# Query convolution in plain fp32, and values of two kv heads on two column halves

## What is computed

```python
qkv = x @ w_qkv.T
q = qkv[..., :LATENT]          # 1024 channels, 16 heads of 64
k = qkv[..., LATENT:LATENT + KV_DIM]   # 256 channels, 4 kv heads
q = _causal_conv1d(_causal_conv1d(q, qc1_w, qc1_b, N_HEADS), qc2_w, qc2_b, 1)
k = _causal_conv1d(_causal_conv1d(k, kc1_w, kc1_b, N_KV), kc2_w, kc2_b, 1)
...
q = _rope(_l2norm(q + 0.5 * k_mean), cos, sin)
k = _rope(_l2norm(k + 0.5 * q_mean) * key_temp, cos, sin)
attn = jax.nn.softmax(jnp.where(causal, q @ kg.T * scale, min), axis=-1)
out = (attn @ vg) @ w_o.T
```

## Time and profile before

| | us |
|---|---|
| median of 3 runs (lowest, highest) | 2850.82 (2847.45, 2856.72) |
| the profiled execution: its time | 2847.88 |
| the profiled execution: its span | 2846.1 |
| PE busy in the span | 2491.1 (88%) |
| DVE, POOL, ACT busy | 1837.2, 1599.9, 1478.0 |
| stage with the query convolution | 157 to 513 |
| attention loop | 528 to 769 |

### The profile page before, as it was taken

The page is one execution under the profiler, slowest core; times in us unless marked ns, Lnnn a source line. Parts: engine busy times, 40 slices in busy tenths (PEclk is TensorE's granted clock), DMA queues, the critical chain, the costliest instruction groups (busy, mean ns, idle before and its releaser), DMA issues. The chain is left out here.

```text
span 2846.1 us, 37992 instructions
## 1 busy us (share of the span) xinstructions
PE 2491.1 (88%) x12920; PEld 1885.0 (66%) x12920; DVE 1837.2 (65%) x3158; ACT 1478.0 (52%) x2851; POOL 1599.9 (56%) x1323
## 2 busy tenths in 40 slices
PE   7977884799799837999999999999999999999948
PEld 3465662444377625887887887877877877877734
DVE  2158755465532455777777778678778778778765
ACT  2212221555232117667668667667766766866703
POOL 0057667444200203776776776777776776777651
PEclk9989996799989958999999999999999999999978
DMA  3013210100110015234334333434334333334210
GB/s 142 0 47 100 74 59 8 60 1 1 47 58 23 34 49 178 92 98 149 104 105 126 111 106 122 129 107 120 111 103 126 109 112 113 118 110 126 76 48 30
DMA packets 143230, 244.00 MB, mean 86 GB/s; under 512 B 28224, under 2 KB 48448, under 8 KB 142784
## 3 DMA queue, kind: packets, MB, share of 16 engines
q1 hardware_dynamic: 143040, 241.58, 27.3%
HBM read 234.18 MB, written 7.34 MB: 85 GB/s over the span
## 5 line engine op out<-in xcount | busy, mean ns | idle before, releaser
L1672 ACT ACTIVATE mix<-mix,sc 128x128 f32<-128x128 f32 x1024 | 310.8, 389 | 5.4 <-DMA mix<-row_cum 5.4
L96 PE MATMUL ps<-s_xt_hi,w_in_hi 128*128 128x512 f32 x640 | 266.9, 417 | 50.2 <-ACT sg L1664 33.3
L1771 DVE SCALAR_TENSOR_TENSOR feat<-ps,chan,feat 128x511 f32<-128x511 f32 (+2 forms) x384 | 283.8, 739 | 10.1 <-ACT feat L1654 8.3
L1883 POOL TENSOR_TENSOR w_in_lo<-w_in_raw,w_in_hi 128x512 fp32r<-128x512 f32 x160 | 216.8, 1355 | 114.9 <-ACT w_in_hi L1629 114.9
L1801 DVE TENSOR_TENSOR y_lo<-y,y_hi 128x512 fp32r<-128x512 f32 x128 | 171.1, 1337 | 162.1 <-ACT y_hi L1688 159.9
L1760 DVE TENSOR_TENSOR mix<-mix,cb 128x512 f32<-128x512 f32 x256 | 271.0, 1063 | 0.0
L1867 POOL TENSOR_TENSOR xend<-xdt,sc 128x384 f32<-128x384 f32 x128 | 106.9, 835 | 280.1 <-DVE xdt L1734 278.5
L98 PE MATMUL ps<-s_xt_hi,w_in_lo 128*128 128x512 f32 x640 | 253.2, 396 | 0.0
L97 PE MATMUL ps<-s_xt_lo,w_in_hi 128*128 128x512 f32 x640 | 251.9, 394 | 0.0
L96 PE MATMUL ps<-s_xt_hi,w_g_hi 128*128 128x512 f32 x512 | 212.0, 414 | 21.1 <-DVE feat L1771 21.0
L1544 PE MATMUL ps<-w_o_hi,y_hi 128*128 128x512 f32 x512 | 207.4, 405 | 5.4 <-DVE y_lo L1801 3.4
(11 more groups left out here) (269 smaller groups left out, 6424.4 us busy)
## 6 DMA issues: line engine op xcount, KB each, us to landing
mix<-row_cum SPq DMA_DIRECT2D x128, 512.0 KB, 5.8
w_in_raw<-in_w_conv_in SPq DMA_DIRECT2D x160, 256.0 KB, 3.1
w_g_raw<-in_w_gate_in SPq DMA_DIRECT2D x128, 256.0 KB, 3.5
ecb<-row_ecum SPq DMA_DIRECT2D x256, 96.0 KB, 3.4
w_o_raw<-in_w_out SPq DMA_DIRECT2D x64, 256.0 KB, 3.0
w<-in_w_c2q SPq DMA_DIRECT2D x16, 768.0 KB, 4.3
w<-in_w_c2q SPq DMA_DIRECT2D x16, 512.0 KB, 3.7
wqkv<-in_w_qkv SPq DMA_DIRECT2D x1, 3072.0 KB, 13.8
```

Of the source, the lines that this page charges most:

```text
L96: pe.matmul(out, a_hi, b_hi, start=(n == 0), stop=False)
L1672: last = act.activation(m, m, ACT.Relu, bias=sc[:, b, CUM, z, 2 * i + e:2 * i + e + 1], scale=-1.0)
L1771: dve.scalar_tensor_tensor(out=to, in0=ps[:, j % 2, 0:S - back], scalar=chan[:, bb % B, j, K1 - 1 - back:K1 - back], in1=to, op0=ALU.mult, ...
L1883: pool.tensor_tensor(w_in_lo[:, n % RING, :, :], w_in_raw[:, n % RING, :, :], w_in_hi[:, n % RING, :, :].bitcast(F32), ALU.subtract).then_ ...
```

## The change

In the second stage each product is one plain fp32 matmul (two records), without parts. The high and low tiles go, and with them ScalarE's whole share of prepare, L551 and L693. Sums of tokens go straight into `tx` (three buffers), mixed taps into `mixed` (three buffers), and the closing products read the loaded taps as they are. There are now three buffers of raw taps, a closing item's one being free when the item is done. The passes run inner n=0, closing n=0, inner n=1, closing n=1, and the first half's rope_q stands earlier: one after every second item from item 18 on. x is no longer used as scratch, and isn't loaded again in the third stage.

In the third stage `values` takes two kv heads, every second iteration: head 2i writes PSUM partitions 0 to 63, head 2i+1 partitions 64 to 127 of the same bank, their matmuls taking turns. There are four buffers of transposed probabilities, and `store` writes for both heads.

```diff
-    RAWS, WS, PAIRS, JT = 2, 3, S // 2, NT // 2
+    RAWS, WS, PAIRS, JT = 3, 3, S // 2, NT // 2
...
-            t_hi = sb("t_hi", [P, WS, 2, B, PAIRS], F32R)
-            t_lo = sb("t_lo", [P, WS, 2, B, PAIRS], F32R)
-            w_hi = sb("w_hi", [P, WS, 2, BANK], F32R)
-            w_lo = sb("w_lo", [P, WS, 2, BANK], F32R)
+            tx = sb("tx", [P, WS, 2, B, PAIRS])
+            mixed = sb("mixed", [P, WS, 2, BANK])
+            ends = sb("ends", [P, 2, BANK])
+            sums = sb("sums", [P, 2, BANK])
...
-            x_flat = x[:, :, :].rearrange("p t d -> p (t d)")
-            ends = x_flat[:, 0:2 * BANK].rearrange("p (i n) -> p i n", i=2)
-            mixed = x_flat[:, 2 * BANK:6 * BANK].rearrange("p (i k n) -> p i k n", i=2, k=2)
-            t_raw = x_flat[:, 6 * BANK:8 * BANK].rearrange("p (k b n) -> p k b n", k=2, b=B)
...
-            INNER = 2 * QT
 
             def inner_item(r):
-                return r < INNER
+                return r // QT % 2 == 0
+
+            def inner_before(r):
+                return r // (2 * QT) * QT + min(r % (2 * QT), QT)
 
...
-                return r // QT, r // QT % 2, r % QT
+                return r // QT, r // QT // 2, r % QT
...
-            ROPE_AT = 3 * QT + 2
+            ROPE_AT = 2 * QT + 2
...
-                    if r >= ROPE_AT:
-                        rope_q(r - ROPE_AT)
+                    if r >= ROPE_AT and r % 2 == 0:
+                        rope_q((r - ROPE_AT) // 2)
...
-                            sp.wait_ge(mixed_done, 2 * (r - RAWS + 1))
+                            sp.wait_ge(mixed_done, 2 * inner_before(r - RAWS + 1))
                         else:
-                            sp.wait_ge(w_low, r - RAWS + 1)
+                            sp.wait_ge(item_done, r - RAWS + 1)
...
-                        pe.wait_ge(w_low, r + 1)
-                        pe.wait_ge(t_low, r + 1)
+                        pe.wait_ge(t_one, r + 1)
+                        pe.wait_ge(t_two, r + 1)
+                        if closing:
+                            pe.wait_ge(w2_loaded[r % RAWS], 16 * (r // RAWS + 1))
+                        else:
+                            pe.wait_ge(mixed_done, 2 * inner_before(r + 1))
                         for j in tiles:
                             b, half = divmod(j, 2)
-                            cols = slice(half * P, (half + 1) * P)
                             if c == 0 and p == 0 and j == 0:
                                 pe.wait_ge(raw_done, NK)
-                            if c == 0 and 1 <= p <= 2:
-                                pe.wait_ge(part_done, 2 * (JT * (p - 1) + j + 1))
-                            if c == 0 and p == 3:
+                            if c == 0 and closing:
+                                pe.wait_ge(part_done, 2 * (JT * n + j + 1))
+                            if c == 0 and p == 2:
                                 pe.wait_ge(final_done, 2 * (j + 1))
                             for kind in range(2):
-                                dst = ps[:, 2 * j + kind, :]
-                                a_hi, a_lo = t_hi[:, r % WS, kind, b, cols], t_lo[:, r % WS, kind, b, cols]
-                                pe.matmul(dst, a_hi, w_hi[:, r % WS, kind, :], start=(c == 0), stop=False)
-                                pe.matmul(dst, a_hi, w_lo[:, r % WS, kind, :], start=False, stop=False)
-                                last = pe.matmul(dst, a_lo, w_hi[:, r % WS, kind, :], start=False,
-                                                 stop=(c == QT - 1 and not closing))
+                                taps = w2[:, r % RAWS, 2 * kind, :] if closing else mixed[:, r % WS, kind, :]
+                                last = pe.matmul(ps[:, 2 * j + kind, :], tx[:, r % WS, kind, b, half * P:(half + 1) * P], taps,
+                                                 start=(c == 0), stop=(c == QT - 1 and not closing))
...
-                        if r >= 1:
-                            dve.wait_ge(t_low, r)
+                        if r >= WS:
+                            dve.wait_ge(item_done, r - WS + 1)
                         if inner_item(r):
-                            dve.tensor_tensor(t_raw[:, 0, :, :], odd[:, :, 0:PAIRS], even[:, :, 1:], ALU.add).then_inc(t_one, 1)
-                            dve.wait_ge(ends_done, r + 1)
-                            if r >= 2:
-                                dve.wait_ge(w_low, r - 1)
+                            dve.tensor_tensor(tx[:, r % WS, 0, :, :], odd[:, :, 0:PAIRS], even[:, :, 1:], ALU.add).then_inc(t_one, 1)
+                            dve.wait_ge(ends_done, inner_before(r + 1))
                             for kind, op in ((0, ALU.add), (1, ALU.subtract)):
-                                dve.tensor_tensor(mixed[:, r % 2, kind, :], ends[:, r % 2, :], w2[:, r % RAWS, 1, :],
+                                dve.tensor_tensor(mixed[:, r % WS, kind, :], ends[:, r % 2, :], w2[:, r % RAWS, 1, :],
                                                   op).then_inc(mixed_done, 1)
-                            src = mixed[:, r % 2, :, :]
                         else:
-                            dve.tensor_tensor(t_raw[:, 0, :, :], even[:, :, 0:PAIRS], even[:, :, 1:], ALU.subtract).then_inc(t_one, 1)
-                            src = w2[:, r % RAWS, 0:TAPS:2, :]
-                        dve.wait_ge(w_high, r + 1)
-                        dve.tensor_tensor(w_lo[:, r % WS, :, :], src, w_hi[:, r % WS, :, :].bitcast(F32),
-                                          ALU.subtract).then_inc(w_low, 1)
+                            dve.tensor_tensor(tx[:, r % WS, 0, :, :], even[:, :, 0:PAIRS], even[:, :, 1:], ALU.subtract).then_inc(t_one, 1)
...
-                        act.activation(t_hi[:, r % WS, :, :, :], t_raw[:, :, :, :], ACT.Copy).then_inc(t_high, 1)
-                        if inner_item(r):
-                            act.wait_ge(mixed_done, 2 * (r + 1))
-                            act.activation(w_hi[:, r % WS, :, :], mixed[:, r % 2, :, :], ACT.Copy).then_inc(w_high, 1)
-                        else:
-                            act.wait_ge(w2_loaded[r % RAWS], 16 * (r // RAWS + 1))
-                            act.activation(w_hi[:, r % WS, :, :], w2[:, r % RAWS, 0:TAPS:2, :], ACT.Copy).then_inc(w_high, 1)
...
-                    schedule(prepare, rope_k, lambda p, j: None, rope_q)
+                    schedule(lambda r: None, rope_k, lambda p, j: None, rope_q)
...
-                        pool.wait_ge(t_high, r + 1)
-                        pool.tensor_tensor(t_lo[:, r % WS, :, :, :], t_raw[:, :, :, :], t_hi[:, r % WS, :, :, :].bitcast(F32),
-                                           ALU.subtract).then_inc(t_low, 1)
+                            pool.tensor_tensor(tx[:, r % WS, 1, :, :], odd[:, :, 1:], odd[:, :, 0:PAIRS], ALU.subtract).then_inc(t_two, 1)
...
-            prob_t = sb("prob_t", [P, 2, ZB, GQ, P])
+            prob_t = sb("prob_t", [P, 4, ZB, GQ, P])
...
-                    def values(u):
-                        b, z, kv = units[u]
-                        if u >= 1:
-                            pe.wait_ge(ot_done, 2 * u)
+                    def values(pair):
+                        b, z, kv = units[2 * pair]
+                        if pair >= 1:
+                            pe.wait_ge(ot_done, 4 * pair)
+                        pe.wait_ge(pt_done, tiles_before[2 * pair + 2])
                         for k in range(z + 1):
-                            pe.wait_ge(pt_done, tiles_before[u] + k + 1)
-                            last = pe.matmul(ps[0:HD, PV_BANK, :], v_tok[:, b * ZB + k, kv * HD:(kv + 1) * HD],
-                                             prob_t[:, u % 2, k, :, :].rearrange("p i n -> p (i n)"),
-                                             start=(k == 0), stop=(k == z))
+                            for e in range(2):
+                                last = pe.matmul(ps[e * HD:(e + 1) * HD, PV_BANK, :],
+                                                 v_tok[:, b * ZB + k, (kv + e) * HD:(kv + e + 1) * HD],
+                                                 prob_t[:, (2 * pair + e) % 4, k, :, :].rearrange("p i n -> p (i n)"),
+                                                 start=(k == 0), stop=(k == z))
                         last.then_inc(pv_ready, 1)
...
-                        if 2 <= u < NU + 2:
-                            values(u - 2)
+                        if u % 2 == 1 and 3 <= u < NU + 3:
+                            values((u - 3) // 2)
...
-                                if u >= 3:
-                                    act.wait_ge(pv_ready, u - 2)
-                                act.activation(prob_t[:, (u - 1) % 2, k, :, :],
+                                if u >= 5:
+                                    act.wait_ge(pv_ready, (u - 5) // 2 + 1)
...
-                    def store(u):
-
-                        b, z, kv = units[u]
+                    def store(pair):
+
```

(16 more changed lines are left out.)

43 lines of the change are left out of this document (17 added, 26 removed).

## The result

The changed kernel takes **2778.66 us** (median of 4 runs, 2777.43 to 2781.88), the kernel before on the same chip 2850.47. The ratio is 0.9747, 95% interval 0.9729 to 0.9765. Predicted were 2773 us, with a range of 2756 to 2793.

The account below looks back on a forecast made before the run. The prediction took preparation, not TensorE's products, to pace the convolution, and TensorE to bound attention nearly everywhere. Gains of 61 us (convolution) and 17 (attention) make 78: 2850.8 - 78 = 2773 us, range 2756 to 2793.

Parts of the forecast that it names:

- The start of the convolution: Convolution: two preparations ahead of the keys end 7 us earlier, item 0 starts at 190.4, a cold clock loses 3 us.
- The preparation at nothing: Convolution: VectorE's 4.15 and GpSimd's 3.8 us an inner item hide under TensorE's 6.87; cost 0, range 0 to 5 us.
- The evictions at nothing: Convolution: PSUM evictions on VectorE, 2.06 us a group, free each group before TensorE returns to it; no stall.
- The end: Convolution's tail: item 28 ends, GpSimd's rn at 409.7, then 42.96 us as before to 452.6; 61 us gained.
- The column halves: Attention: two heads' value products run side by side in column halves, taking 34 us of TensorE's time away.
- Rival 1: Attention: products in the two column halves don't overlap, a loss of 18 us there; time 2808 us, chance 0.07.
- The floor of an even iteration: Attention: exponentials, then copies of transposed probabilities, keep even four-tile iterations from going below 7.63 us.
- rival 3: Attention: the copies of L884 behind the exponentials set every iteration and take all its gain; 2790 us, chance 0.06.
- Attention's sum: Attention: 10.4 us gained in the second sequence, 5.4 in the first, 1 behind the last unit; about 17, bounds 10 to 30.
- The 57%: Attention: share of moved work kept as gain, 2.04 of 3.6 us in iteration 18, applied to the whole second sequence.
- rival 4: Convolution: TensorE's clock falls to 1.2 GHz, each item costs 6.87 us more; 2990 us with all 32, chance 0.02.
- The wait as cover: Attention, first sequence: iterations 2, 4 and 6 lack a projection (1.8 us) as cover, so 5 us less is gained.

Follow-up runs that it names:

- filler: Changed kernel plus three unused plain fp32 products ahead of TensorE's wait in each of attention iterations 2, 4 and 6: 2772.44 us, ratio 0.9723.

## Why the prediction was right, and where it wasn't

**The start of the convolution.** Item 0 was put at 190.4 and came at 191.19. Eight items from there took 57.22 us, 2.3 over 8 x 6.87; 3 were allowed for the cold start.

**The item.** 6.87 us, as read from other plain products.

**The preparation at nothing.** Right. No product waits for `mixed` or `tx`, and no rotation made a stall. Only one wait was missed: 0.65 us for the raw taps of item 31. I had said that a closing item's taps are free two items before they are wanted. That doesn't hold in the tail, where the last three items are done group by group: their first group comes at once behind item 28, whose buffer the last one needs.

**The evictions at nothing.** Right; no wait for them is left of 19.8 us. The run with the preparation kept still had 15.1, and the one with the light preparation and the old order of passes has none, so it was VectorE's load that caused them.

**The end.** Item 28 ended at 399.5 (88 records from 365.14 on, the first 80 of them up to it), GpSimd's rn came at 409.78 (409.7 predicted), the next stage's first copy at 452.85 (452.6). The step that carried most of the gain, reading the tail as one fixed piece of 43 us behind the first group, held to 0.1 us. Behind it 0.8 us went again: the low clock reaches 5.7 us into the third stage's transposes (until 458.5), against 3.7 us before.

**The column halves.** They overlap, 16 records in 3.65 us. Rival 1 is out. Why turns are better than one head after the other the prediction didn't ask.

**The floor of an even iteration.** 7.63 us predicted, 7.54 measured. The Trainium skill's rule that tiling TensorE doesn't speed up the evacuation of PSUM ("Trainium Kernel Development and Optimization", Best Practices) shows as this floor; its strict reading, nothing gained (rival 3), does not hold: the even iterations 18 to 28 had work above the floor.

**Attention's sum.** This is the step that failed. By sequence: the second gained 10.5 us (10.4 predicted), the part behind the last unit 0.6 (1.0), the first *lost* 2.0, where a gain of 5.4 was predicted.

In the second sequence the number came out by luck. The 57% was one iteration's share, applied to all. In fact the eight even iterations (16 to 30) are 14.4 us shorter together, 78% of the 18.4 moved, and three odd ones are longer at full clock: 17 by 1.3, 27 by 0.5 and 29 by 2.0 us. That an odd iteration loses nothing was wrong: the exponentials and copies bind there too once the even one is shorter. In 17 the scores are drawn out over 3.94 us (1.99 before), and in 27 and 29 TensorE waits 0.37 and 0.58 us for ScalarE's copy ahead of the values. The two errors cancel.

The missing 7.4 us in the first sequence is the clock. The spells cost 0.7, 1.5, 2.4 and 1.6 us in iterations 3, 5, 7 and 13, and iterations 2, 4 and 6 are another 1.4 us longer than with filler. I priced the clock only in the convolution (rival 4), where the change fills TensorE, and not in attention, where it empties it. The text had both halves of it: that the clock "fell where TensorE idled", and a floor of 7.63 us under an even iteration whose TensorE work would be less, which is to say that TensorE would idle there. I didn't join the two.

**The wait as cover.** Where I wrote that iterations 2, 4 and 6 "have no projection as cover and keep that much less", that was right in size at full clock: with filler the first sequence gains 4.1 us, though iteration 13 still has its spell. With the spell's 1.6 us this makes 5.7, an estimate beside the 5.4 predicted.

**Sum.** Predicted 61 + 17 = 78. Measured in the trace 59.8 + 9.2 = 69; the medians say 71.8. The time stayed in the range although attention's part lay below its own bound of 10: the 8 us missing there are little beside a range of 37.

## What to carry to other kernels

Where preparation and not TensorE sets the pace, the cheaper arithmetic is not the one with the shorter product: the plain fp32 product costs TensorE 25% more, and the change to it took 58 us from the kernel (the new order of passes included) because little had to be prepared for it. Work taken off TensorE in a loop whose floor is another engine's chain turns into waits, in the neighbouring iterations too, and waits can cost clock: read the granted clock of both parts of such a loop, and try work, even useless work, in the waits before taking more out. A stage that ends 7 us sooner may lose most of that if the next one's clock falls differently, as here (5.1 us), so compare stages before whole times. And before calling an iteration slow by the clock, look whether the granted clock fell in it: iteration 13 takes 6.9 us at full clock.

## What the runs showed of the hardware

- Spells at half clock came back at the same iterations with the same lengths in two executions (31 iterations within 0.02 us), and fell elsewhere when the same loop began 7 us later. They are not noise, and not a property of the loop alone.
- Three useless products in each of three waits made the loop 6.3 us shorter (231.4 to 225.1 us).
- Products in different column halves of one bank, both accumulating over four key tiles, run at the same time: starts 6 to 7 ns apart, 0.43 us from one to the next in a half, 16 records in 3.65 us. With all products of one half first, the starts show the overlap beginning when four of its records are left, for pairs of four, three and two key tiles.
- The state-space block, the same code in the same place of the program, took 1768.8 to 1778.7 us in executions of one kernel.
